# Loads moved ahead of the phases that use them, and the first attention group worked off in two query halves

## The chip, the cores and the metric

One core of a Trainium2 chip runs the whole program. The metric is the device time of one execution in microseconds (us), the median of three. Five engines work side by side: TensorE (PE; its weight loads are PEld), VectorE (DVE), ScalarE (ACT), GpSimd (POOL) and SyncE (SP), which here issues nearly all transfers. ACT can issue transfers too, on a queue of its own.

## The reference

Four sequences of 1024 tokens, 256 wide, in float32. Two layers, each a mixer and a feed-forward part; what matters here is the first layer:

```
# L0 attention, 16 heads of 16, causal, with an ALiBi slope for each head
att = softmax(q @ k.T / 4 + slope * tril(j - i) + causal)     # 1024 x 1024 for each head and sequence
x1  = x + (att @ v) @ W_proj + b_proj
# L0 ffn: two layers, each
h   = shift_token(z);  q, k, v = split(h @ wqkv)              # 8 heads of 64
q, k = rotary_xpos(l2norm(q) * q_scale, l2norm(k) * k_scale)
z1  = z + local_attention(q, k, v) @ wo                       # 128 queries see their block and the one before
h   = shift_token(z1);  a, g = split(layernorm(h) @ w1 + b1)
z   = z1 + (a * gelu(g)) @ w2 + b2
```

After it come the second layer's selective scan (a front of projections and a convolution, then the scan) and a mixture of 32 experts. Before each part stands a normalisation.

## The kernel before, in words

The kernel is a row of phases, each with on-chip buffers, semaphores and a block of its own: `phase_qkv` (A), `phase_attention` (B), then twice `phase_window` (D) and `phase_feed_forward` (E), then `phase_front` (F), `phase_scan` (H) and `phase_moe` (I). Tiles carry the letter of their phase in the profile (`B_probs`, `D_rope`). Between two phases all engines meet at a barrier, and what one phase hands to the next lies in device memory (`z`, `z1`, `q_parts`). So a phase can load its weights and its first tokens only after the barrier, and computes nothing till they are there.

Attention (B). Queries and keys are split into three bfloat16 parts, stacked on 96 partitions, with 4 more rows for the slopes and for the shift of the softmax. One group is 4 heads of one sequence; there are 16 groups. `load(g)` (lines 601 to 608) issues 17 transfers on SP: 12 of 128 KB for q and k, two of rows, the values (`v_raw`), `centre` and `key_bias`. All 17 count on one semaphore, so nobody starts on a group before its last transfer. A group has 48 units of maxima (`score` on PE, `reduce_max` on DVE, line 750) and 48 units of exponentials (`score_T` on PE, line 907, `Exp` on ACT, line 852). The exponentials need the row maxima as a shift: after the group's 48th maximum DVE works them out (`shifts`), PE turns them (`turn`, line 895), ACT copies them (line 844), and SP copies 4 rows for each head into `q` (`put_shift`, line 614). Every engine works its list strictly in order: PE does the 48 maxima of group 0 alone; from then on it takes an exponential unit and, beside it, the maxima of the next group, which keep a lead of up to 16. The shift of group g + 1 is turned before exponential 36 of group g. Every four exponentials PE also weighs the values (`weigh`, line 925). Two transposed halves of each group's result are stored as `yT` (line 626) and projected at fixed places, for sequence 2 before exponential 39 of group 11 (`project`, line 887; it waits for the stores of both halves it reads).

SP's list in B: `load(0)`, `load(1)`, `load(2)`, `put_shift(0)`, and then for each g: `load(g + 3)`, now and then x, the stores of `yT`, `put_shift(g + 1)`, and the stores of x1 and z.

Local attention (D) works 32 tiles of 128 tokens. At its start SP loads tiles 0 to 2, `ident`, `band`, `rope` and `wo`, ACT issues `wqkv` and `factor`. GpSimd builds the masks (lines 1124 to 1128) and multiplies all 8 blocks of the rotary table by the scales (line 1132) before it takes up the inverse norms of tile 0 (line 1137), which scale k (line 1181), which PE then turns (line 1358). In the steady part SP stores tile i and then loads tile i + 4.

Feed-forward (E) works 8 chunks of 512 tokens. SP loads chunk 0 first, then weights and chunk 1. In the first layer's E, `clear` (10 MB of zeros to `slots_x`) goes out on ACT's queue.

The front (F) starts with ACT waiting for all small weights, because it negates `dt_b` (line 2100) ahead of its first copy of the transposed tokens (line 2046).

## Time and profile before

| | |
|---|---|
| median of 3 runs | 3671.98 us (3669.59 to 3672.42) |
| the profiled execution: its own time, its span | 3675.01 us, 3673.2 us |
| mean granted clock of TensorE, share of full | 0.948 |
| TensorE, VectorE, ScalarE, GpSimd busy | 88%, 67%, 50%, 39% |
| attention's first matmul and last projection | 144.07 us, 740.8 us |
| D, E, D, E, F: first matmul | 757.2, 1271.3, 1532.4, 2048.1, 2310.4 us |

The span is from the first to the last instruction of the core. A start of a phase is seen as a stretch in which TensorE does nothing.

### The profile page before, as it was taken

The numbers are of one execution on the slowest core, as the hardware profiler recorded it, in microseconds if no ns is written. First come the engines' busy times: TensorE is split into PE (matmuls) and PEld (weight loads), VectorE is DVE, ScalarE is ACT, GpSimd is POOL, SyncE is SP. The second block draws the span as 40 slices with busy tenths as digits, with TensorE's granted clock in tenths as the row PEclk, the third lists the DMA queues.
The fourth block names the chain that finished last, engine by engine and source line by source line (L and its number), as shares of the span: only waits on it lengthen the run. The fifth ranks groups of instructions, "written<-read, shape, count | busy, mean of one in ns | idle before, by whom it ended". The sixth has DMA issues, their size and how long they took to land. (4 is left out here: it accounts for less than half of the span.)

```text
span 3673.2 us, 52297 instructions
## 1 busy us (share of the span) xinstructions
PE 3235.6 (88%) x18096; PEld 1975.8 (54%) x18096; DVE 2455.5 (67%) x4653; ACT 1849.0 (50%) x3943; POOL 1432.4 (39%) x993
## 2 busy tenths in 40 slices
PE   8599999879999799799999799798288888887798
PEld 4244444346666555466666455333256565655676
DVE  8488888547777422277777232398599999996633
ACT  2176776736666411166666211355377777774100
POOL 4101111122222211122222111134599999996533
PEclk9699999989999899899999899899699999999899
DMA  5956575120000241100000321343525151512873
GB/s 170 150 68 92 80 96 79 34 67 25 23 23 23 91 145 46 58 23 23 23 23 20 94 69 46 96 152 144 212 83 201 58 201 58 201 58 88 294 229 118
DMA packets 275715, 347.29 MB, mean 95 GB/s; under 512 B 70976, under 2 KB 206640, under 8 KB 274812
## 3 DMA queue, kind: packets, MB, share of 16 engines
q1 hardware_dynamic: 259596, 305.70, 30.5%
q10 hardware_dynamic: 10736, 25.94, 2.0%
q0 software_dynamic: 5120, 12.30, 0.9%
q8 instruction: 145, 2.38, 0.3%
q14 instruction: 118, 0.97, 0.1%
HBM read 227.72 MB, written 112.80 MB: 93 GB/s over the span
## 5 line engine op out<-in xcount | busy, mean ns | idle before, releaser
L2414 POOL TENSOR_TENSOR H_feed<-H_ndu,H_bs 128x1024 f32<-128x1024 f32 x256 | 595.6, 2372 | 7.0 <-DMA H_cs<-between_bc 4.0
L852 ACT ACTIVATE B_probs<-B_p_exp,B_key_bias 128x512 f32<-128x512 f32 (+3 forms) x768 | 394.8, 583 | 143.2 <-PE B_p_exp L910 112.8
L750 DVE TENSOR_REDUCE B_part_max<-B_p_max 128x1 f32<-128x512 f32 (+3 forms) x768 | 374.7, 546 | 83.3 <-PE B_p_max L874 80.8
L1286 ACT ACTIVATE D_probs<-D_scores,D_neg,D_rq 128x256 f32<-128x256 f32 x512 | 283.1, 573 | 255.7 <-DVE D_neg L1198 255.7
L2385 ACT ACTIVATE H_decay<-H_ndt,H_rate 128x1024 f32<-128x1024 f32 x256 | 287.9, 1125 | 198.7 <-DVE H_turning L2467 103.1
L871 PE MATMUL B_p_max<-B_k,B_q 100*128 100x512 bf16 (+3 forms) x768 | 256.7, 341 | 43.8 <-DMA B_key_bias<-in_key_bias 33.7
L1696 PE MATMUL E_p_ag<-E_hT,E_w 128*128 128x512 f32 x640 | 282.8, 601 | 2.1 <-ACT E_hT L1652 2.1
L2467 DVE TENSOR_TENSOR_SCAN H_turning<-H_decay,H_feed 128x1024 f32<-128x1024 f32 x112 | 253.5, 2275 | 22.9 <-POOL H_feed L2414 22.7
L2518 PEld LDWEIGHTS H_p_y<-H_minus,H_sT 128*128 128x128 f32 x1792 | 225.1, 200 | 75.6 <-ACT H_sT L2370 55.6
L2518 PE MATMUL H_p_y<-H_minus,H_sT 128*128 128x128 f32 x1792 | 233.5, 287 | 35.8 <-ACT H_sT L2370 35.8
L907 PE MATMUL B_p_exp<-B_q,B_k 100*128 100x512 bf16 (+3 forms) x768 | 250.1, 329 | 11.4 <-ACT B_probs L852 6.5
L1137 POOL TENSOR_TENSOR D_rnorm<-D_norm,D_power 128x8 f32<-128x8 f32 x64 | 106.2, 1659 | 380.3 <-DVE D_norm L1153 380.3
L1668 ACT ACTIVATE E_gated<-E_p_ag,E_b 128x512 f32<-128x512 f32 x96 | 62.6, 652 | 373.1 <-PE E_p_ag L1696 353.9
L2370 ACT ACTIVATE H_sT<-H_p_T,H_cT 128x128 f32<-128x128 f32 x896 | 242.9, 388 | 11.1 <-PE H_p_T L2508 11.0
L1341 PE MATMUL D_p_qk<-D_wqkv,D_hT 128*128 128x512 f32 x512 | 243.1, 618 | 1.1 <-ACT D_hT L1261 1.1
L1195 DVE CUSTOM_DVE_ANT_0 D_scores<-D_scores,D_mask 128x256 f32<-128x256 f32 x512 | 202.0, 457 | 56.0 <-PE D_scores L1368 55.7
L2467 DVE TENSOR_TENSOR_SCAN H_decay<-H_decay,H_feed 128x1024 f32<-128x1024 f32 x96 | 218.9, 2281 | 16.7 <-POOL H_feed L2414 16.6
L1141 POOL TENSOR_TENSOR D_rnorm<-D_norm,D_power 128x8 f32<-128x8 f32 x64 | 106.7, 1667 | 286.7 <-DVE D_norm L1153 286.7
L1696 PEld LDWEIGHTS E_p_ag<-E_hT,E_w 128*128 128x128 f32 x640 | 121.9, 192 | 155.2 <-issue 154.2
L1623 DVE SCALAR_TENSOR_TENSOR E_act_out<-E_p_ag,E_b,E_gated 128x512 f32<-128x512 f32 x96 | 67.7, 706 | 196.5 <-ACT E_gated L1668 196.5
L871 PEld LDWEIGHTS B_p_max<-B_k,B_q 100*128 100x128 bf16 x768 | 75.2, 98 | 221.5 <-DVE B_part_max L750 133.0
L2526 PE MATMUL H_p_y<-H_part,H_minus 128*128 128x512 f32 x384 | 184.5, 603 | 9.1 <-DVE H_part L2443 9.0
(269 smaller groups left out, 6857.8 us busy)
## 6 DMA issues: line engine op xcount, KB each, us to landing
H_bs<-between_bc SPq DMA_DIRECT2D x64, 512.0 KB, 7.7
H_cs<-between_bc SPq DMA_DIRECT2D x36, 512.0 KB, 8.4
B_q<-between_q_parts SPq DMA_DIRECT2D x96, 128.0 KB
B_k<-between_k_parts SPq DMA_DIRECT2D x96, 128.0 KB
between_slots_x<-E_clear ACTq DMA_DIRECT2D x4, 2570.0 KB
I_xe<-between_slots_x ACTq DMA_DIRECT2D x32, 257.0 KB, 4.0
D_base<-between_z SPq DMA_DIRECT2D x64, 128.0 KB
between_z<-D_z SPq DMA_DIRECT2D x64, 128.0 KB
```

The costliest lines, as they stand in the source:

```text
L750: nc.vector.reduce_max(part_max[:, g % 2, kc, qb, h:h + 1], p_max[:, use % 3, 0:keys], AX.X).then_inc(maxed, 1)
L852: nc.scalar.activation(probs[:, x % PROBS, skip:512], p_exp[:, n % SCORES, skip:512], ACT.Exp, bias=key_bias[:, g % SETS, kb - 4 * Q + 4, ...
L871: last = nc.tensor.matmul(p_max[:, use % 3, 0:keys], q[0:KR, u, h, qb * P:(qb + 1) * P], k[0:KR, u, h, 512 * kc:512 * kc + keys], start=Tr ...
L907: last = nc.tensor.matmul(p_exp[:, n % SCORES, skip:512], k[0:KR, u, h, kb * P:(kb + 1) * P], q[0:KR, u, h, 512 * Q + skip:512 * Q + 512], ...
L1286: last = nc.scalar.activation(probs[:, place[m], :, :].rearrange("p a b -> p (a b)"), scores[:, place[m], :, :].rearrange("p a b -> p (a b ...
L1341: last = nc.tensor.matmul(p_qk[:, m, :], hT[:, i % 2, k, :], wqkv[:, k, m * INNER:(m + 1) * INNER], start=k == 0, stop=k == KD - 1)
L1696: last = nc.tensor.matmul(p_ag[:, m % 2, n, :], w1[:, k, at:at + P], hT[:, i % 2, k, :], **flags)
L2370: last = nc.scalar.activation(sT[:, k % 2, h * HB + b, :], p_T[:, h, b, :], ACT.Copy, scale=cT[:, i % 2, h * HB + b, s:s + 1])
L2385: nc.scalar.activation(decay[:, n % 2, :], ndt[:, g % 2, :], ACT.Exp, scale=rate[:, m, s:s + 1]).then_inc(decayed, 1)
L2414: nc.gpsimd.tensor_tensor(feed[:, n % AHEAD, :], ndu[:, g % 2, :], bs[:, s, :], ALU.mult).then_inc(fed, 1)
L2467: nc.vector.tensor_tensor_scan(out, decay[:, n % 2, :], feed[:, n % AHEAD, :], 0.0, ALU.mult, ALU.add).then_inc(scanned, 1)
L2518: last = nc.tensor.matmul(p_y[:, h, b * P:(b + 1) * P], sT[:, k % 2, h * HB + b, :], minus[:, :], start=False, stop=False)
```

## The change

It has three parts.

1. Loads ahead. Two new classes own the buffers of D's and of E's weights and first tokens (`LocalAhead`, `FeedAhead`), which now outlive a phase. D's list (11 weight transfers and tiles 0 to 2) is issued by SP during attention, after `put_shift(11)`, and for the second layer after chunk 3 of E. E's list (18 weight transfers and chunks 0 and 1) is issued by SP in D after the store of tile 16. The waits at a phase's start are for these semaphores. In D GpSimd now does block 0 of the rotary table first, and the other seven, two at a time, after the inverse norms of tiles 0 to 3. In E the memset of `clear` comes after the first inverse deviation.
2. Group 0 of attention. q goes on SP's queue and k on ACT's, each as two halves of 512 tokens, with a semaphore for each half, and the values between the halves of q. PE starts at the first half. Only 24 maxima come first: 16 of the first query half (`OWN`), whose shift is made at once, and 8 of the second. Then come `turn`, the 16 exponentials of the first half with the other 24 maxima beside them, the second `turn`, and the 32 exponentials of the second half with two maxima each beside them. SP's list begins: group 0, `load(1)`, `put_half(0)`, `load(2)`, `put_half(1)`. The shift of group 1 is turned before exponential 44 of group 0 (`LATE_TURN`) and no longer before 36.
3. In F GpSimd negates `dt_b`, and ACT waits for it at its first `put_xs`.

```diff
-        stream = [("turn", 0, 0), ("turn", 0, 1)]
+        EARLY, OWN, LATE_TURN = 24, 4 * GH, 44
+        stream = [("turn", 0, 0)]
         for g in range(NG):
             for e in range(NE):
-                if e == TURN and g + 1 < NG:
+                if g == 0 and e == OWN:
+                    stream.append(("turn", 0, 1))
+                if e == (TURN if g else LATE_TURN) and g + 1 < NG:
                     stream += [("turn", g + 1, 0), ("turn", g + 1, 1)]
...
         def max_target(g, e):
             at = NE * g + e + 1
+            if g == 0:
+                return EARLY + 3 * at // 2 if e < OWN else NM + 2 * (at - OWN)
             return min(NG * NM, NM + at + min(LEAD, at * LEAD // NE))
...
+            def load_first():
+                for half, done in ((0, first_half), (1, second_half)):
+                    cols = slice(512 * half, 512 * half + 512)
+                    for n, part in enumerate((0, 0, 1, 1, 0, 2)):
+                        sp.dma_start(q[HD * n:HD * n + HD, 0, :, cols], ...).then_inc(done, 16)
+                    if half == 0:
+                        sp.dma_start(q[96:KR, 0, :, :], T["q_rows"]).then_inc(done, 16)
+                        values(0)
+            def put_half(half):
+                sp.wait_ge(exped, (turned[0] if half else 0) + 1)
+                for h in range(GH):
+                    sp.dma_start(q[96:KR, 0, h, 512 * half:512 * half + 512], shift_rows[32 * h:32 * h + 4, 0, half, :]
+                                 ).then_inc(q_shifted, 16)
...
-            load(0)
+            load_first()
             load(1)
+            put_half(0)
             load(2)
-            put_shift(0)
+            put_half(1)
...
+                if g == NG - 6:
+                    sp.wait_ge(first_row, 16)
+                    sp.wait_ge(z_stored[0], 16)
+                    local.load(sp, T, 0)
...
# phase_window, SP
+                if i == TILES // 2:
+                    sp.wait_ge(first_row, 16)
+                    for u in range(2):
+                        sp.wait_ge(stored[u], 16 * 4)
+                    feed.load(sp, T, layer)
# phase_window, GpSimd
-            pool.wait_ge(rope_loaded, 16 * 7)
-            for b in range(BLOCKS):
-                nc.gpsimd.tensor_tensor(rope[:, b, :, :], rope[:, b, :, :], factor[:, :, :], ALU.mult
-                                        ).then_inc(rope_ready, 1)
             for i in range(TILES):
                 inverses(i)
+                for b in range(2 * i + 1, min(2 * i + 3, BLOCKS)):
+                    tables(b)
...
# phase_feed_forward, SP
+                if i == 3 and not last_layer:
+                    sp.wait_ge(stored[0], 16)
+                    local.load(sp, T, layer + 1)
...
# phase_front
+            nc.gpsimd.tensor_scalar(dt_b[:, :], dt_b[:, :], -1.0, None, ALU.mult).then_inc(bias_ready, 1)
-            act.wait_ge(small_loaded, 16 * (TAPS + 3 + XT))
-            nc.scalar.mul(dt_b[:, :], dt_b[:, :], -1.0).then_inc(bias_ready, 1)
-            act.wait_ge(bias_ready, 1)
```

## Rows read from the trace of the kernel before

**Rows 1.** Sums by window: length, busy of PE, PEld, DVE, ACT, POOL, clock, DMA, GB/s.

```profile
110.30:144.10 33.80, 0.08 (x2) 0.06 (x2) 2.05 (x5) 0.00 (x0) 6.75 (x6) 0.57 0.98 162
174.90:218.20 43.30, 39.93 (x292) 18.34 (x293) 31.98 (x70) 27.28 (x51) 1.05 (x1) 0.90 0.48 58
...
1518.80:1532.40 13.60, 0.03 (x3) 0.04 (x1) 1.22 (x1) 0.00 (x0) 1.17 (x4) 0.60 0.52 180
```

**Rows 2.** Timeline of the start of D, first layer: start, length, instruction, idle before.

```profile
748.73 0.36 SPq L1097 DMA_DIRECT2D D_ident<-in_ident  x1
757.23 0.45 PE L1333 MATMUL D_p_hz<-D_ident,D_base 128*128 128x128 f32 x1 [16.39 <-DMA D_before<-between_z]
762.86 0.69 DVE L1153 TENSOR_REDUCE D_norm<-D_square 128x8 f32<-128x512 f32 x1 [18.11 <-ACT D_square L1266]
764.06 5.96 POOL L1132 TENSOR_TENSOR D_rope<-D_rope,D_factor 128x256 f32<-128x256 f32 x8 [3.04 <-DMA D_factor<-in_k_scale]
769.98 1.63 POOL L1137 TENSOR_TENSOR D_rnorm<-D_norm,D_power 128x8 f32<-128x8 f32 x1
772.07 0.69 DVE L1181 TENSOR_TENSOR D_kr<-D_ksum,D_rnorm 128x512 f32<-128x512 f32 x1 [4.67 <-POOL D_rnorm L1139]
777.71 3.53 PE L1368 MATMUL D_scores<-D_qkT 64*128 64x256 f32 x16 [1.19 <-ACT D_qkT L1277]
```

**Rows 3.** Timeline of the starts of E, both layers: first issue, first statistics.

```profile
1259.70 0.37 SPq L1528 DMA_DIRECT2D E_h<-between_z  x1
1266.36 1.41 DVE L1604 BATCH_NORM_STATS2 E_stats<-E_h 128x6 f32<-128x256 f32 x4 [9.53 <-DMA E_h<-between_z]
2036.79 0.38 SPq L1528 DMA_DIRECT2D E_h<-between_z  x1
2043.12 1.41 DVE L1604 BATCH_NORM_STATS2 E_stats<-E_h 128x6 f32<-128x256 f32 x4 [9.20 <-DMA E_h<-between_z]
```

**Rows 4.** Timeline of the start of F.

```profile
2310.41 1.09 PE L2135 MATMUL F_p_T<-F_ident,F_xn 128*128 128x128 f32 x4 [13.99 <-DVE F_xn L1973]
2316.32 0.59 ACT L2046 COPY F_xT<-F_p_T 128x512 f32<-128x512 f32 x1
```

**Rows 5.** Timeline of group 0 of attention: group 1's values, shift rows, first exponential.

```profile
160.85 0.61 POOL L685 COPY B_v<-B_v_raw 128x512 f32<-128x512 f32 x1 [16.25 <-DMA B_key_bias<-in_key_bias]
170.93 2.61 SPq L614 DMA_DIRECT2D B_q<-B_shift_rows  x4
175.62 0.69 ACT L852 ACTIVATE B_probs<-B_p_exp,B_key_bias 128x512 f32<-128x512 f32 x1 [4.72 <-PE B_p_exp L910]
```

**Rows 6.** Sums by window, maxima alone (line 750): length, DVE busy, clock, DMA, GB/s.

```profile
144.10:168.00 23.90, 23.06 (x48) 0.57 1.14 127
188.40:218.20 29.80, 20.77 (x44) 0.94 0.23 21
```

**Rows 7.** Stores of yT, issue to landing, from 226 to 245 us and from 577 to 580 us.

```profile
DMA to landing us min/median/max: 2.4/6.1/10.2
...
L626 SPq DMA_DIRECT2D B_yT<-B_yn x4: 507/590/594, 577.2 to 579.0; - x4
DMA to landing us min/median/max: 2.0/2.2/2.4
```

**Rows 8.** Timeline: shift rows of group 11, first load of group 14, projection for sequence 2.

```profile
551.03 2.50 SPq L614 DMA_DIRECT2D B_q<-B_shift_rows  x4
559.50 0.35 SPq L601 DMA_DIRECT2D B_q<-between_q_parts  x1
584.33 1.51 PE L887 MATMUL B_p_max<-B_w,B_yT 128*128 128x256 f32 x6
```

**Rows 9.** Transfers of the stretch from 749 to 767 us.

```profile
DMA packets 4304, 4.26 MB, mean 237 GB/s; under 512 B 1104, under 2 KB 4048, under 8 KB 4304
```

**Rows 10.** Timeline in the steady part of D: a tile's load, and PE taking up a tile.

```profile
1033.20 0.43 SPq L1090 DMA_DIRECT2D D_base<-between_z  x1
1055.34 0.27 PE L1333 MATMUL D_p_hz<-D_ident,D_base 128*128 128x128 f32 x1
```

More of the change, by code:

```diff
@@ L574, in phase_attention @@
         max_use, unit_use = {}, {}
-        for n in range(NM):
+        for n in range(EARLY):
             max_use[n] = n
@@ L838, in _ @@
         def _(act):
+            for half, done in ((0, first_half), (1, second_half)):
+                cols = slice(512 * half, 512 * half + 512)
+                for n, part in enumerate((0, 1, 0, 1, 2, 0)):
+                    act.dma_start(k[HD * n:HD * n + HD, 0, :, cols], T["k_parts"][part_rows(0, part), cols]
+                                  .rearrange("(h d) t -> d h t", h=GH)).then_inc(done, 16)
+                if half == 0:
+                    act.dma_start(k[96:KR, 0, :, :], T["k_rows"][0:4, :, :]).then_inc(done, 16)
             for n, (kind, g, at) in enumerate(stream):
@@ L891, in turn @@
             def turn(n, g, half):
-                pe.wait_ge(shift_ready, g + 1)
+                pe.wait_ge(shift_ready, g + 2 if g else half + 1)
                 reached(pe, exped, n - SCORES + 1)
@@ L1078, in starts @@
             return i % BLOCKS == 0
-        def loads(i):
-            return sum(3 if starts(j) and j else 2 for j in range(i % 4, i + 1, 4))
         @block.sync
@@ L1508, in reached @@
                 eng.wait_ge(sem, value)
-        def starts(i):
-            return i % PER_SEQ == 0
-        def loads(i):
-            return sum(4 if starts(j) else 2 for j in range(i % 2, i + 1, 2))
         rest_transfers = 2 if last_layer else 1
@@ L1589, in _ @@
                 if i == 0:
-                    pool.wait_ge(b2_loaded, 16 * CT)
+                    if not last_layer:
+                        nc.gpsimd.memset(clear[:, :], 0.0).then_inc(clear_ready, 1)
+                    pool.wait_ge(feed.weights, WEIGHTS)
                 pool.wait_ge(rest_loaded[u], 16 * rest_transfers * (i // 2 + 1))
@@ L3065, in tables, with __init__, total, loads @@
             **attention_tables(), **rope_tables(), **slot_tables()}
+class LocalAhead:
+    WEIGHTS = 11
+    def __init__(self, nc, ctx):
+        sb = lambda name, shape: ctx.enter_context(nc.sbuf_tensor(f"LA_{name}", shape, F32))
+        self.ident = sb("ident", [P, P])
+        self.band = sb("band", [P, 2, P])
+        self.wqkv = sb("wqkv", [P, KD, 3 * INNER])
+        self.wo = sb("wo", [P, INNER // P, DIM])
+        self.factor = sb("factor", [P, 4, LD])
+        self.rope = sb("rope", [P, SEQ // P, 4, LD])
+        self.base = sb("base", [P, 4, DIM])
+        self.before = sb("before", [P, 4, P])
+        self.weights = nc.alloc_semaphore("LA_weights")
+        self.loaded = [nc.alloc_semaphore(f"LA_loaded_{u}") for u in range(4)]
+    def total(self, i):
+        return sum(3 if j % (SEQ // P) == 0 and j else 2 for j in range(i % 4, i + 1, 4))
+    def loads(self, layer, i):
+        return layer * self.total(TILES - 4 + i % 4) + self.total(i)
+    def load_tile(self, sp, T, i):
+        u, tok = i % 4, i * P
+        sp.dma_start(self.base[:, u, :], T["z"][tok + 1:tok + 1 + P, :]).then_inc(self.loaded[u], 16)
+        if i % (SEQ // P) == 0 and i:
+            sp.dma_start(self.before[1:P, u, :], T["z"][tok + 1:tok + P, P:DIM]).then_inc(self.loaded[u], 16)
+            sp.dma_start(self.before[0:1, u, :], T["zeros"][0:1, 0:P]).then_inc(self.loaded[u], 16)
+        else:
+            sp.dma_start(self.before[:, u, :], T["z"][tok:tok + P, P:DIM]).then_inc(self.loaded[u], 16)
+    def load(self, sp, T, layer):
+        sp.dma_start(self.ident[:, :], T["ident"][:, :]).then_inc(self.weights, 16)
+        sp.dma_start(self.band[:, :, :], T["band"].rearrange("a p n -> p a n")).then_inc(self.weights, 16)
+        sp.dma_start(self.wqkv[:, :, :], T["wqkv"][layer].rearrange("(k p) n -> p k n", p=P)).then_inc(self.weights, 16)
+        sp.dma_start(self.rope[:, :, :, :].rearrange("p b a d -> p b (a d)"),
+                     T["rope"][0:SEQ, :].rearrange("(b p) n -> p b n", p=P)).then_inc(self.weights, 16)
+        for n, name in enumerate(("q_scale", "k_scale")):
+            row = T[name][layer:layer + 1, :]
+            sp.dma_start(self.factor[:, 2 * n, :], row.broadcast_to([P, LD])).then_inc(self.weights, 16)
+            for side in range(2):
+                here, other = side * HALF_D, (1 - side) * HALF_D
+                sp.dma_start(self.factor[:, 2 * n + 1, here:here + HALF_D],
+                             row[:, other:other + HALF_D].broadcast_to([P, HALF_D])).then_inc(self.weights, 16)
+        sp.dma_start(self.wo[:, :, :], T["wo"][layer].rearrange("(k p) n -> p k n", p=P)).then_inc(self.weights, 16)
+        for i in range(3):
+            self.load_tile(sp, T, i)
```

267 lines of the change are left out of this document (136 added, 131 removed).

## The prediction

> **What bounds the kernel now.** I read the page first: TensorE is busy for 88% of the span, so in the steady stretches its list sets the pace, and time can be had only where it stands still. So I looked for the stretches without a matmul, and summed the engines over them by window. Between A and attention TensorE does nothing for 33.8 us, ahead of the second D for 13.6 us [rows 1]; the starts of the first D, both E and F look like the latter. In these windows TensorE's granted clock averages 0.57 to 0.60, so the work that follows starts at the lower level of 1.2 GHz. Then I read the timelines of these starts for what ended last. At D it is the transfer of the first tokens: the block's first issue is at 748.73, the first matmul at 757.23 [rows 2]. At E it is the chunk of tokens that DVE waits for: 1259.70 to 1266.36, and 2036.79 to 2043.12 [rows 3]. In attention it is first the 17th transfer of group 0, then the lone maxima, which keep DVE busy for 23.06 of 23.90 us (0.48 us each) while TensorE waits on it [rows 6], then the turn of the shift.
>
> **The starts of D.** After the change weights and tiles are on the chip at the barrier. I take TensorE's first matmul 0.45 us after the block's first instruction: 757.23 - 748.73 - 0.45 = 8.0 us gained. Behind it lies a second wait. GpSimd multiplies eight table blocks, 764.06 to 770.02, before the inverse norm that was ready to be worked at 763.55 (762.86 + 0.69); k is scaled at 772.07 [rows 2]. Now one block is done before the norm arrives, so the inverse starts at 763.6 instead of 769.98, 6.4 us earlier on the same scale. TensorE must first finish the projection of v and the turn of tile 1, which costs some 0.2 us of that, and I take off as much again for DVE: 6.0 us. From k's scaling to the first scores it is 5.6 us either way (777.71 - 772.07). So 14.0 us for this D. The second has the same list; its idle stretch of 13.6 us [rows 1] is shorter than the first's 16.4 [rows 2] only by what lies ahead of the barrier, so again 14.0. Bounds for a D: 8 (the table work hides nothing) and 18 (TensorE keeps the upper clock through the shortened gaps and saves a few us on the first tile). The cover for the seven later blocks is GpSimd's idle time in tiles 0 to 3: two blocks are 2 x 0.75 = 1.5 us (5.96 / 8 each) in a tile of some 15 us (32 tiles from 777.71 to 1259.70 [rows 2 and 3]); without it they would cost 6 us.
>
> **The starts of E.** 1266.36 - 1259.70 = 6.7 and 2043.12 - 2036.79 = 6.3 us of waiting, less 0.1 each for DVE's own start: 12.8 us together [rows 3]. Bounds 10 and 15. The memset of `clear` now comes behind the first inverse; ACT, which waits for it after its first `hT`, has nothing else to do before the first product: 0, at most 2 us.
>
> **F.** ACT's first copy of the transposed tokens starts at 2316.32, though TensorE was done at 2310.41 + 1.09 = 2311.50. It had waited for the small weights. Gain 4.8 us [rows 4]; the negation on GpSimd is one 128 x 4 instruction and is needed much later. Bounds 2 and 5.
>
> **What pays for it: the lists on SP's queue.** In attention, D's list follows `put_shift(11)`, issued from 551.03 for 2.50 us, so begins at about 553.6, and stands ahead of `load(14)`, issued from 559.50 [rows 8]. Transfers of one queue land behind one another: the stores of yT issued right behind a group's load needed up to 10.2 us to land, those issued on a drained queue 2.0 to 2.4 us [rows 7]. The list is 4.0 MB. At the 237 GB/s with which the same list came in at D's start [rows 9] it needs 16.7 us, at best some 13, so it is through at 567 to 571. Group 14's load then begins 7 to 11 us late, and behind it come the yT stores of group 11's first half, which the projection at 584.33 waits for [rows 8]. They landed at 579.0 + 2.2 = 581.2, so 3.1 us of the delay is slack: a stall of 4 to 8 us. I take 5. Bounds 0 (the queue drains faster) and 12. Next behind it is `put_shift(12)`, which has 10 us.
>
> In D, E's list (4 MB, 24 transfers) stands ahead of one tile's load. A load issued at 1033.20 is for the tile that TensorE takes up at 1055.34 [rows 10], 22.1 us later. The list takes 13 to 17 us by the rate above and lands some 4 us before it is missed: nothing, with up to 5 us for each D as the other bound. D's list in E has a chunk of 32 us as cover: nothing.
>
> **Group 0 of attention.** Before: maxima from 144.1 to 168.0 [rows 6], SP's shift issues at 170.93, first exponential 175.62 [rows 5], so the turn costs 7.6 us; the group's exponentials and 64 maxima end at 218.2 [rows 1]. After: the first half of q and k is 0.8 MB, so that at 127 GB/s [rows 6] and with other traffic between, PE starts at about 131 and has the 24 maxima by 144. Their shift is at SP by 146. But SP's list has `load(1)` ahead of `put_half(0)`, and group 0 and 1 together bring the same bytes as before. The last transfer of group 1 landed at 160.85 [rows 5], and the shift rows land right behind it, by the queue's behaviour above. First exponential at about 161.5. Its 16 exponentials with 24 maxima take 14 us (12.8 before, with 21 maxima [rows 6]); at 175.6 comes a second turn of 6.7 us (half the rows to turn and copy), since nothing else is listed for TensorE there; exponential 16 starts at 182.3. Then 64 maxima at 0.487 us are 31.2 us of DVE, with 2.5 us of its other work and start: 216. DVE, not TensorE, is the bound here, as the 20.8 us for 44 maxima already hint [rows 6]. The late turn of group 1 leaves only four exponentials of cover and costs 1 us. End 217 against 218.2: I count 2 us gained, since two queues may bring group 1 a little earlier. Bounds: if the rows landed at once, at 149, exponential 16 would wait for group 2's load (about 174) and the group would end at 208, 10 us gained; if the DVE-bound part stretches like before's (29.8 us for 44 maxima), 5 us lost.
>
> The Trainium skill ("DMA: Bandwidth & Descriptors", "Rules for kernel authors") says that a second issuing queue brings no bandwidth, since all run on the same 16 engines. No row here shows two queues on these 16-partition transfers. By that rule group 1 still lands at 160.85 and this term is 1 us; if two queues did double the rate for their 0.8 MB, it would be 3 to 4 us.
>
> **The sum.** D 28.0, E 12.8, F 4.8, group 0 2.0, together 47.6; less the stall of 5.0 is 42.6. For fewer stretches at the lower clock in D I add 1.4, which is the middle of 0 and some 3: 44.0. The profiled execution took 3675.0, which gives 3631.0; the median lies 3.0 below it, so 3628.
>
> **Rivals.** (a) The shift rows do not wait behind `load(1)` (few rows, few engines), and yT neither: group 0 gains 10 and there is no stall, 13 more: 3615. For it: in calm stretches such rows land within 4 us. Against: the 10.2 us [rows 7]. (b) D gains only its first wait, since TensorE or DVE is late anyway before the first scores: 12 less, 3640. The row of 5.96 us [rows 2] speaks against it. (c) Queues bite deeper: 12 us at the projection, 5 at each D's list: 17 less, 3645. The 22.1 us against 17 speak against it, narrowly. (d) Slower: D's list clogs SP's queue in attention. The stall is the list's end less 559.5 less 3.1 us; it eats the 49 us of all gains once the list ends at 612, that is at under 70 GB/s over 58 us. Were it to last 65 us, the time would be 3679. Rows 9's 237 GB/s for the same transfers is against it. (e) No change, because the starts only move the wait to the first tile's or chunk's next transfer: 3672; against it stands that all of the first three tiles are in the list.
>
> **How the numbers follow.** Forecast 0.56, (a) 0.14, (b) 0.12, (c) 0.12, (d) 0.03, (e) 0.03. The forecast's own spread is 3619 to 3637; 3612 to 3643 takes in (a), (b) and most that lies between, leaving about 2 in 10. What this kernel's measurement can tell from no change is 0.2%, 7 us: faster 0.94, same 0.03, slower 0.03.
>
> **What the profile after would show.** In D: the first matmul within 1 us of the block's first instruction, one `D_rope` instruction before the first `D_rnorm`, and the first scores some 14 us after the first matmul (20.5 before). In E: statistics at once. In F: the copy right behind the transposes. In attention: maxima at 131, first exponential near 161 with SP's shift issues at 146, a second hole of 6 to 7 us before exponential 16, DVE over 90% busy from 183 to 216; and a hole of about 5 us in front of the projection in group 11. Wrong would be: shift rows landing at 149, no hole at the projection, or tiles 19 to 21 of D waiting for their tokens.

## The result: faster, by less than forecast

The changed kernel takes 3646.0 us (median of 5 runs, 3636.7 to 3651.4), the kernel before 3672.0 us (5 runs, 3669.6 to 3679.1): a ratio of 0.9926, with a 95% interval of 0.9907 to 0.9944. The forecast was 3628 us with a range of 3612 to 3643, so the sign was right and the time lay 3 us outside the range. The profiled execution went from a span of 3673.2 to 3644.2 us: 29 us gained where 44 were forecast. By the medians the gain is 26 us, since before the change the profiled execution lay 3.0 us above its median, and after it the profiled execution is the median.

First what came out as forecast. These are lines of the timeline of the changed kernel: the start of the first D, the first E, the second E, and F. They answer to [rows 2], [rows 3] and [rows 4].

```profile
755.71 0.45 PE L1364 MATMUL D_p_hz<-LA_ident,LA_base 128*128 128x128 f32 x1 [8.12 <-PEq L83]
756.76 0.72 POOL L1160 TENSOR_TENSOR LA_rope<-LA_rope,LA_factor 128x256 f32<-128x256 f32 x1
...
761.54 1.64 POOL L1175 TENSOR_TENSOR D_rnorm<-D_norm,D_power 128x8 f32<-128x8 f32 x1 [2.68 <-DVE D_norm L1193]
...
769.26 3.36 PE L1399 MATMUL D_scores<-D_qkT 64*128 64x256 f32 x14 [1.19 <-ACT D_qkT L1308]
...
1254.96 1.40 DVE L1585 BATCH_NORM_STATS2 E_stats<-FA_h 128x6 f32<-128x256 f32 x4 [2.86 <-PEq L83]
...
1258.32 4.38 POOL L1570 MEMSET E_clear<- 128x5140 f32 x1
1262.66 2.37 POOL L1573 TENSOR_TENSOR E_rest<-E_rest,FA_b 128x1024 f32<-128x1024 f32 x1
...
1258.40 7.43 DVE L1597 TENSOR_SCALAR E_hn<-FA_h,E_mean_var,E_rstd 128x256 f32<-128x256 f32 x4 [1.62 <-POOL E_rstd L1567]
...
1265.98 1.94 PE L1663 MATMUL E_p_T<-FA_ident,E_hn 128*128 128x128 f32 x8 [14.34 <-DVE E_hn L1597]
...
2021.05 1.38 DVE L1597 TENSOR_SCALAR E_hn<-FA_h,E_mean_var,E_rstd 128x256 f32<-128x256 f32 x4 [1.61 <-POOL E_rstd L1567]
...
2022.58 1.73 PE L1663 MATMUL E_p_T<-FA_ident,E_hn 128*128 128x128 f32 x7 [8.27 <-DVE E_hn L1597]
...
2283.83 1.09 PE L2113 MATMUL F_p_T<-F_ident,F_xn 128*128 128x128 f32 x4 [14.38 <-DVE F_xn L1952]
...
2284.96 0.58 ACT L2025 COPY F_xT<-F_p_T 128x512 f32<-128x512 f32 x1 [25.28 <-PE F_p_T L2113]
```

Ahead of the first D TensorE stands still for 8.12 us in place of 16.39, and from its first matmul to the first scores it is 769.26 - 755.71 = 13.55 us in place of 20.48. In F the copy follows the transposes at once. In both E the statistics start with the block. But the idle stretch ahead of E falls only in the second: 8.27 us there, 14.34 in the first. There the four `E_hn` instructions took 7.43 us and not 1.38, over nearly the same time (1258.40 to 1265.83, against 1258.32 to 1265.03) in which GpSimd fills `clear` and adds to `rest`.

Second, the two lists on SP's queue. Timeline lines of D's list in attention, then of E's list in the first D, each with the first matmul that came late by it:

```profile
554.17 2.07 SPq L3083 DMA_DIRECT2D LA_wqkv<-in_wqkv  x1
...
567.83 0.43 SPq L635 DMA_DIRECT2D B_q<-between_q_parts  x1
...
579.08 9.52 SPq L662 DMA_DIRECT2D B_yT<-B_yn  x8
...
590.04 3.32 PE L944 MATMUL B_p_max<-B_w,B_yT 128*128 128x256 f32 x7 [5.91 <-issue]
...
1024.49 0.33 SPq L3141 DMA_DIRECT2D FA_ident<-in_ident  x1
...
1037.53 5.19 SPq L3131 DMA_DIRECT2D FA_h<-between_z  x1
...
1044.07 0.74 SPq L3073 DMA_DIRECT2D LA_base<-between_z  x1
...
1048.88 0.33 PE L1364 MATMUL D_p_hz<-LA_ident,LA_base 128*128 128x128 f32 x1 [2.23 <-DMA LA_before<-between_z]
```

Group 14's load is issued at 567.83, 8.3 us later than in [rows 8], and the stores of yT begin 11.3 us later, since SP also took 2.9 us longer over the load and x. SP is busy with the eight stores for 9.52 us, but 5.10 of them are the first store alone, and the same store held SP for 4.94 us in the kernel before. The changed kernel, then the kernel before:

```profile
579.08 5.10 SPq L662 DMA_DIRECT2D B_yT<-B_yn  x1
```
```profile
567.82 4.94 SPq L626 DMA_DIRECT2D B_yT<-B_yn  x1
```

The last four stores go out from 586.2 to 588.0 (577.2 to 579.0 in [rows 7]: 9.0 us later) and land 1.9 to 2.3 us after their issue, so the last one at about 590.0. The projection starts at 590.04, after a wait of 5.9 us. The profile names no releaser for this wait ("issue"); that it is the stores follows from this landing and from the second experiment. Once issued, the stores land as fast as on a drained queue. The view of the DMA issues from 577 to 590 us (number, KB each, median us from issue to landing) has them:

```profile
B_yT<-B_yn SPq DMA_DIRECT2D x8, 32.0 KB, 2.3
```

In D, SP needs from 1024.49 to 1044.07 for E's list, 5.19 us of it for one single transfer. The load of tile 20 stands behind it: it is issued at 1044.07, and TensorE, which asks for the tile at 1048.88 - 2.23 = 1046.65, waits for 2.2 us.

Third, group 0 of attention, in timeline lines and in the sums by window (length, then busy time with the number of instructions of PE, PEld, DVE, ACT, POOL, then clock, DMA share, GB/s). They answer to [rows 5] and [rows 6].

```profile
142.00 0.59 ACT L897 CAST B_shift_rows<-B_p_exp 128x512 bf16<-128x512 f32 x1 [34.73 <-PE B_p_exp L952]
142.61 2.61 SPq L651 DMA_DIRECT2D B_q<-B_shift_rows  x4
...
153.30 0.61 POOL L726 COPY B_v<-B_v_raw 128x512 f32<-128x512 f32 x1 [18.74 <-DMA B_key_bias<-in_key_bias]
...
155.06 0.61 PE L966 MATMUL B_p_exp<-B_q,B_k 100*128 100x512 bf16 x1 [13.10 <-DMA B_q<-B_shift_rows]
...
172.54 0.58 ACT L897 CAST B_shift_rows<-B_p_exp 128x512 bf16<-128x512 f32 x1 [3.08 <-PE B_p_exp L952]
...
176.78 0.61 PE L966 MATMUL B_p_exp<-B_q,B_k 100*128 100x512 bf16 x1 [4.27 <-DMA B_q<-B_shift_rows]
```
```profile
130.10:142.00 11.90, 9.28 (x48) 4.03 (x48) 10.83 (x28) 0.01 (x1) 0.61 (x1) 0.64 1.11 165
142.00:155.80 13.80, 0.74 (x3) 0.39 (x4) 0.00 (x0) 0.58 (x1) 0.61 (x1) 0.50 1.03 117
155.80:177.40 21.60, 14.35 (x98) 6.27 (x97) 13.99 (x28) 8.80 (x17) 0.00 (x0) 0.82 0.40 40
177.40:216.50 39.10, 35.25 (x229) 15.12 (x227) 30.55 (x68) 19.93 (x34) 1.05 (x1) 0.85 0.46 63
```

The first scores come 13.10 us, and exponential 16's 4.27 us, behind a turn, with TensorE idle. Group 1's first exponential stands at 218.4 us, where it stood before (218.2). In the stretches that hold or follow the two holes TensorE's granted clock is 0.50 and 0.82 to 0.85, that is wholly or in part 1.2 GHz.

From the first exponential to group 1's first it is 62.6 us (155.8 to 218.4), and was 42.5 before (175.62 to 218.17). The new order lost the 20 us that the earlier start had won.

### The profile page after: what moved, and what is told of

Read it like the earlier page. It is cut to its first block and busy times, and to the rows that moved or that the text cites. A ratio compares the mean times of both kernels' runs of the same rounds, so it can differ in the third digit from the quotient of the medians.

```text
span 3644.2 us, 52320 instructions
## 1 busy us (share of the span) xinstructions
PE 3237.4 (89%) x18096; PEld 1980.4 (54%) x18096; DVE 2456.9 (67%) x4657; ACT 1848.5 (51%) x3942; POOL 1430.8 (39%) x992
## 5 line engine op out<-in xcount | busy, mean ns | idle before, releaser
L1677 PE MATMUL E_p_ag<-E_hT,FA_w 128*128 128x512 f32 x640 | 283.8, 603 | 1.9 <-ACT E_hT L1633 1.9
L928 PE MATMUL B_p_max<-B_k,B_q 100*128 100x512 bf16 (+3 forms) x768 | 254.6, 338 | 34.2 <-DMA B_q<-in_q_rows 20.1
L1649 ACT ACTIVATE E_gated<-E_p_ag,FA_b 128x512 f32<-128x512 f32 x96 | 62.5, 651 | 373.6 <-PE E_p_ag L1677 354.4
L1372 PE MATMUL D_p_qk<-LA_wqkv,D_hT 128*128 128x512 f32 x512 | 240.2, 612 | 0.9 <-ACT D_hT L1292 0.9
L1677 PEld LDWEIGHTS E_p_ag<-E_hT,FA_w 128*128 128x128 f32 x640 | 122.1, 193 | 155.7 <-issue 152.0
L1604 DVE SCALAR_TENSOR_TENSOR E_act_out<-E_p_ag,FA_b,E_gated 128x512 f32<-128x512 f32 x96 | 67.8, 707 | 199.4 <-ACT E_gated L1649 199.4
```

Source lines behind the costliest of these rows:

```text
L928: last = nc.tensor.matmul(p_max[:, use % 3, 0:keys], q[0:KR, u, h, qb * P:(qb + 1) * P], k[0:KR, u, h, 512 * kc:512 * kc + keys], start=Tr ...
L1372: last = nc.tensor.matmul(p_qk[:, m, :], hT[:, i % 2, k, :], wqkv[:, k, m * INNER:(m + 1) * INNER], start=k == 0, stop=k == KD - 1)
L1677: last = nc.tensor.matmul(p_ag[:, m % 2, n, :], w1[:, k, at:at + P], hT[:, i % 2, k, :], **flags)
```

## The experiments

Times of single profiled executions are given where only a stretch matters. Kernels of one group ran on one chip. Beside them the kernel before had medians of 3689.9 (one run), 3677.5 (7) and 3680.4 (7), so whole times are compared only within a group, and stretches across all traces. The first six experiments have one execution each: 3637.1, 3641.1, 3637.6 and 3625.1 us (memset behind `hn`; list two groups later; list in four; maxima first) beside 3689.9, and 3636.0 and 3643.2 (rows by ACT; tables at once) beside 3677.5.

**E's memset behind `hn`.**

```diff
                 if i == 0:
                     if not last_layer:
+                        pool.wait_ge(hn_ready, 1)
                         nc.gpsimd.memset(clear[:, :], 0.0).then_inc(clear_ready, 1)
```

> The kernel after, with one wait more: in the first E, GpSimd fills `clear` only after DVE has written the first `hn` (it waits for `hn_ready`), and adds `b2` to `rest` behind that. In the kernel after, the four `hn` instructions of the first E took 7.43 us (1258.40 to 1265.83) with GpSimd's memset of `clear` (1258.32, 4.38 us) and its add (1262.66, 2.37 us) over the same time; in the second E, without a `clear`, they took 1.38. Theory A (GpSimd's work beside it slows DVE): `hn` takes 1.4 us, the idle stretch of TensorE ahead of the first E falls from 14.3 to 8.3 us, like the second E's. Theory B (something else is slow in the first E, as its transfers of `rest` that land then): `hn` stays at about 7.4 us and the stretch at 14.3. By A the time is 6 us under the kernel after, by B the same. The memset ends some 1.5 us later than before the edit, with ACT's first product not yet there: nothing.

The view of one source line (duration in ns as min/median/max, first and last start) of the changed kernel, and then of this one:

```profile
L1597 DVE TENSOR_SCALAR E_hn<-FA_h,E_mean_var,E_rstd x4: 400/1410/4444, 1258.4 to 1265.4; 128x256 f32<-128x256 f32 x4
```
```profile
L1598 DVE TENSOR_SCALAR E_hn<-FA_h,E_mean_var,E_rstd x4: 406/407/413, 1256.1 to 1257.0; 128x256 f32<-128x256 f32 x4
```

TensorE's idle stretch is 8.29 us: theory A, to the tenth. Narrower windows of the same view have the four one by one: the first, 4.44 us, is as long as the memset (4.38), the second, 2.42, as long as the add (2.37), and the last two take 0.40 each, when GpSimd is through (it ends at 1265.03, they at 1265.83). So they did not run evenly slower beside GpSimd: the first two stood as long as GpSimd's instructions lasted.

**D's list two groups later.**

```diff
-                if g == NG - 6:
+                if g == NG - 4:
```

> The kernel after, with D's list issued behind the shift rows of group 13 (g of 12) in place of group 11's. In group 12 and 13 no projection waits for stores that lie behind it until group 15, and no load of a group follows. Theory A (the list on SP's queue holds the yT stores back): the idle stretch of 5.9 us ahead of the projection in group 11 goes, the 32 last exponentials of group 11 take 25.7 us as before in place of 33.9, and attention ends 8 us earlier, unless the shift rows or stores of groups 13 and 14 become late (up to 3 us). Theory B (the stall has another origin, such as the projection's own place after the early loads): it stays, and attention ends as in the kernel after. By A 8 us under the kernel after, by B the same.

Theory A. TensorE waits for no issue in that stretch, group 11's exponentials from number 16 on take 27.0 us up to group 12's first, as before (35.2 in the changed kernel), and groups 12 to 15 take what they took (37.4, 32.1, 30.2, 29.3). From group 1's first exponential to the last of attention it is 8.1 us less than in the changed kernel.

**E's list in four parts.** Each `load` of the list takes a part; parts 0 to 3 are issued behind the stores of tiles 16 to 19.

```diff
-                if i == TILES // 2:
+                if TILES // 2 <= i < TILES // 2 + feed.PARTS:
...
-                    feed.load(sp, T, layer)
+                    feed.load(sp, T, layer, i - TILES // 2)
```

> The kernel after, with E's list in both D cut in four: identity, gains and w1 at tile 16, b1, w2 and b2 at tile 17, chunk 0 at tile 18, chunk 1 at tile 19. In the kernel after tile 18 of each D took 18.55 and 18.38 us where all others take 14.87 to 15.2, and SP issued the list from 1024.49 to 1044.07. Theory A (the list ahead of tile 20's load is too long): both tiles go back to 14.9 us, 7 us in all, since the longest part has 1.7 MB and takes under 10 us of the 22 that a tile's load has. Theory B (the same bytes in any pieces slow the tiles' transfers): tiles 18 to 22 together still lose 3 to 4 us for each D. By A 7 us under the kernel after, by B the same.

Theory A: tile 18 takes 14.9 us in both D, and TensorE waits for no tile. From the first scores to the end D takes 477.7 and 477.2 us, in the changed kernel 482.4 and 480.9. That is 8.4 us, of which the two tiles are 7.2; the rest lies within the scatter of a D (480.4 and 477.5 us for the second one in two traces of the kernel before).

**Group 0's maxima first.** 16 maxima, turn of the first half, 32 maxima, turn of the second half, exponentials.

```diff
-        EARLY, OWN, LATE_TURN = 24, 4 * GH, 44
+        EARLY, OWN = 48, 4 * GH
...
-                if g == 0 and e == OWN:
+                if g == 0 and e == 0:
                     stream.append(("turn", 0, 1))
...
             put_half(0)
-            load(2)
             put_half(1)
+            load(2)
```

> The kernel after, with group 0's exponentials no longer between the maxima of its second half: TensorE makes 16 maxima, the turn of the first half's shift, the other 32 maxima, the turn of the second half, and then exponentials with one or two maxima of group 1 each, by the order of the kernel before. SP has both halves' shift rows ahead of group 2's load. Loads of group 0 stay early and in two halves. Theory A (the hole of 13.1 us that TensorE has while the first rows are under way is where maxima are to be made, and DVE's list of 88 maxima behind the first exponential is what took the gain back): maxima end at 130.1 + 48 x 0.49 = 153.6, the first exponential is still at 156 since its rows land no earlier, exponential 16 about 13 us later, as before, and the first exponential of group 1 at 156 + 42.6 = 198 to 202, against 218.4 in the kernel after and 218.2 before: 16 to 20 us gained. Theory B (group 1 and its values land too late, or the later groups take it back because TensorE waits for group 2's load, now issued about 11 us later): under 8 us gained at the end of group 2.

Sums by window, to the first exponential, to exponential 16, to group 1's first:

```profile
142.00:158.60 16.60, 14.03 (x49) 4.03 (x50) 14.79 (x33) 0.56 (x2) 0.61 (x1) 0.50 0.42 45
158.60:170.60 12.00, 11.81 (x93) 6.05 (x90) 8.89 (x20) 8.10 (x17) 0.00 (x0) 0.88 0.76 96
170.60:201.00 30.40, 25.77 (x197) 10.56 (x198) 23.97 (x53) 18.79 (x35) 1.05 (x1) 1.00 1.04 110
```

Theory A: group 1 starts at 201.0, 17.4 us earlier, and keeps it to the end of attention. DVE now works 14.79 us in the hole in which it did nothing, so 44 maxima and not 64 are left beside the last 32 exponentials, and TensorE runs them at the full granted clock (1.00 against 0.85). How much of the gain the clock is, no run separates; in [rows 6] the same 44 maxima took 29.8 us at 0.94, here 30.4 at 1.00. This is nearly the order of the kernel before, begun earlier: the first exponential stands at 158.6 in place of 175.6, and 42.4 us (42.5 before) lie between it and group 1's first.

**Rows issued by ACT.**

```diff
                     nc.scalar.copy(shift_rows[...], p_exp[...]).then_inc(exped, 1)
+                    if n == 0:
+                        act.wait_ge(exped, 1)
+                        for h in range(GH):
+                            act.dma_start(q[96:KR, 0, h, 0:512], shift_rows[...]).then_inc(q_shifted, 16)
```

> The kernel after, with the first half's four shift-row transfers of group 0 issued by ACT, behind its own copy, and no more by SP behind group 1's load. All else stands, the second half's rows by SP behind group 2's load too. In the kernel after they were issued at 142.61 and TensorE took up the first scores at 155.1. Theory A (the rows queue behind group 1's load, which is on the same queue): from ACT's queue, empty since 130, they land 2 to 4 us after their issue and the first exponential comes at 146 to 149, in place of 155.8. Exponential 16 then waits for the second half's rows behind group 2's load, at 172 to 177, and group 1's first exponential comes at 214 to 219: little or nothing gained in the sum. Theory B (the 16 DMA engines are full with group 1's bytes whatever the queue, busy share 1.03 from 142 to 155.8): the rows land near 153 again and the first exponential stays at 155.

Timeline lines: ACT's issue, GpSimd's copy that waits for the last transfer of group 1, the first exponential.

```profile
142.86 2.55 ACTq L903 DMA_DIRECT2D B_q<-B_shift_rows  x4
...
155.27 0.61 POOL L726 COPY B_v<-B_v_raw 128x512 f32<-128x512 f32 x1 [19.74 <-DMA B_key_bias<-in_key_bias]
158.60 0.69 ACT L912 ACTIVATE B_probs<-B_p_exp,B_key_bias 128x512 f32<-128x512 f32 x1 [15.78 <-PE B_p_exp L976]
```

Theory A falls. From a queue of its own the 4 KB rows still land behind group 1's load, and now, it seems, behind a part of group 2's too, which SP issues from 141.56: the first exponential is 3 us later than with the rows from SP's queue, where theory B had it at the same time. Group 1's first exponential comes at 221.4.

**All tables at once.** GpSimd makes D's eight products ahead of the tiles, as before; the loads stay early.

```diff
-                for b in range(2 * i + 1, min(2 * i + 3, BLOCKS)):
-                    tables(b)
...
+            for b in range(BLOCKS):
+                tables(b)
```

> The kernel after, with all eight products of D's tables on GpSimd at once before the tiles, as in the kernel before; the early loads stay. It tells how much of D's gain comes from the order of the tables: in the kernel after, first matmul to first scores is 13.55 us, in the kernel before 20.5. Theory A (both parts of the prediction's term hold, 8 for the loads and 6 for the tables): first matmul still 0.2 us behind the block's start, first scores 19 to 20.5 us behind the first matmul, so 6 to 7 us lost for each D, 13 in all. Theory B (with the tables on the chip at the barrier GpSimd is through with them before it is missed): under 3 us lost for each D, since it starts 8 us earlier on the scale of the block.

```profile
754.85 5.52 POOL L1160 TENSOR_TENSOR LA_rope<-LA_rope,LA_factor 128x256 f32<-128x256 f32 x8 [0.18 <-issue]
760.32 2.09 POOL L1176 TENSOR_TENSOR D_rnorm<-D_norm,D_power 128x8 f32<-128x8 f32 x1
```

Theory B: first matmul to first scores is 768.50 - 752.22 = 16.28 us, 2.7 more than in the changed kernel (2.2 in the second D), and not 6 to 7. The eight products start 2.6 us behind the first matmul, in the kernel before 6.8 (764.06 - 757.23), since their tables are there.

**The kernel before again.**

> The kernel before once more, for a second trace of it. The last stage, whose code the change does not touch, took 284.0 us from its first to its last matmul in the one trace of the kernel before, and 287.1 to 288.3 us in five traces of kernels with the change. Theory A (this is the scatter of that stage, and the one trace was a lucky one): 286 to 289 us here. Theory B (the change moves something that this stage depends on): 284 us again.

The last stage took 284.8 us here: below the 286 to 289 of theory A. But twelve traces of kernels with the change or a part of it have 284.3 to 288.3, so theory B, by which the change sets the higher value, does not hold either. That is mostly scatter; that both traces of the kernel before are at its lower end may be chance. In this trace the first E, which had taken 247.6 us, took 256.7, so a single profiled execution can be 9 us off.

**The mends together, and a tighter order for group 0.** Besides the three mends: eight maxima behind the first turn, two with each exponential, the second turn ahead of exponential 12, first rows by ACT, second rows ahead of group 2's load.

```diff
-        EARLY, OWN, LATE_TURN = 24, 4 * GH, 44
+        EARLY, OWN, SECOND, LATE_TURN = 24, 4 * GH, 12, 40
...
-                return EARLY + 3 * at // 2 if e < OWN else NM + 2 * (at - OWN)
+                return EARLY + 2 * at if e < SECOND else min(NM + 2 * (at - SECOND), 112)
```

> The kernel after with the three mends together (`clear` behind `hn`; D's list behind group 13's shift rows; E's list in four parts) and a new order for group 0: 16 maxima, the turn of the first half, 8 maxima while its rows are under way (issued by ACT), exponentials 0 to 11 with two maxima each, the turn of the second half ahead of exponential 12 (rows by SP ahead of group 2's load), and two maxima with each exponential from there until 64 are made. Theory A (the mends are worth 6 + 8 + 7 us, and group 0 lost its gain to the two holes and the slow stretch after the second): the first exponential near 145, no hole before exponential 16 over 2 us, the first exponential of group 1 at 188 to 196, so 22 to 30 us for group 0; in all 43 to 51 us under the kernel after, 3595 to 3605. Theory B (DVE bounds group 0 from 130 on, 112 maxima at 0.49 us and its other work, with slower maxima while TensorE is at the lower clock): group 1's first exponential at 200 or later, no better than with the maxima first (201.0), and in all 3605 to 3615.

3612.0 us (4 runs, 3610.8 to 3614.3), ratio to before 0.9818 (0.9786 to 0.985). Theory B by both its numbers, with group 1's first exponential at 208.2. That DVE bounds the stretch is not shown: from 171.0 to 208.2 it was busy for 29.79 of 37.2 us. The rows, issued at 139.77, let the first exponential start at 149.39, behind the last transfer of group 1 once more (GpSimd's copy at 147.91), and the order with exponentials between is 7 us slower than the maxima first.

**Group 0 as before, the early loads kept.** Its load, maxima, turn and exponentials are the code of the kernel before.

```diff
-            load_first()
+            load(0)
             load(1)
-            put_half(0)
             load(2)
-            put_half(1)
+            put_shift(0)
```

> The kernel after with group 0 of attention wholly as in the kernel before (one load of 17 transfers on SP's queue, 48 maxima, one turn of both halves, then exponentials with maxima of group 1 alone). The early loads of D and E, E's and F's changes stay. In the traces the first exponential of group 1 stands at 218.2 before and at 218.4 after, whatever happened ahead of it. Theory A (the new order of group 0 gains nothing): group 1's first exponential at 217.5 to 218.5, the time within 3 us of the kernel after run beside it, so all of the 26 us come from the early loads. Theory B (the new order helps somewhere later, as by the state in which it leaves the queues): over 5 us slower than the kernel after.

**The mends with the maxima first**, and the same with its second turn three exponentials later:

```diff
-                if g == 0 and e == 0:
+                if g == 0 and e == 3:
                     stream.append(("turn", 0, 1))
```

> The three mends of the early loads (`clear` behind `hn`; D's list behind group 13's shift rows; E's list in four parts) with group 0's 48 maxima first, the second 32 in the first rows' hole. In single runs the parts were worth 6.0, 8.2, 7.2 and 17.4 us. Theory A (they add up): 38.8 us under the kernel after run beside it, group 1's first exponential at 201, attention's last exponential 26 us earlier than in the kernel after. Theory B (they share something, as a stall that moves): under 32 us.

> The kernel of the row above, with the turn of group 0's second half listed ahead of exponential 3 in place of exponential 0. With the maxima first, the first half's rows had landed at 151.8, but the first exponential stood behind the turn, whose copy was at 158.04. Theory A (the list alone held it): first exponential at 155.5 to 156.5 in place of 158.6, group 1's first exponential 2 to 3 us earlier, so 198 to 199. Theory B (DVE bounds the stretch, or the turn's wait for DVE's shift only moves behind exponential 2): group 1's first exponential at 200 to 201, the time as the row above within 1 us.

> The kernel after, unchanged, on the same chip as the three others, so that they can be compared with it: 3636 to 3651 by its five runs. Its trace tells how far the stall of 5.9 us ahead of group 11's projection (group 11's last 32 exponentials took 33.9 us with it; 28 to 36 us in traces of kernels that have the same list at the same place) and the last stage's 287.1 us scatter. Theory A (both are scatter of transfers): 28 to 36 and 284 to 288. Theory B (fixed by the program): 34 and 287 again.

These four ran on one chip, 4 runs each:

| kernel | median us | range | ratio to before, 95% |
|---|---|---|---|
| changed kernel again | 3644.6 | 3644.0 to 3645.1 | 0.9909, 0.9877 to 0.9941 |
| group 0 as before | 3638.1 | 3636.2 to 3643.0 | 0.9893, 0.986 to 0.9927 |
| mends, maxima first | 3606.4 | 3604.7 to 3607.3 | 0.9806, 0.9774 to 0.9838 |
| and turn at 3 | 3607.4 | 3605.7 to 3609.0 | 0.9809, 0.9777 to 0.9841 |

With group 0 as before, group 1 starts at 219.3 (220.1 in the changed kernel beside it), and the kernel is no slower: the gain of the change comes from its early loads and F's edit. It is even 6.5 us faster, where theory A allowed 3, and the ranges of the four runs do not touch. In the traces the difference lies mostly in places that the edit does not touch: 4.0 us in the stall of group 11 and 3.3 in the first D, both of which scatter from trace to trace. Whether the new order of group 0 has a part in it, as by the times at which it leaves the queues, stays open; it gained nothing. The mends add up: 38.2 us under the changed kernel, 38.8 expected. That they agree so well is in part luck, since two of the parts, the stall and the late tiles, scatter by more than that. The changed kernel's second trace has 36.4 us for group 11's exponentials from number 16 on (35.2 in the first) and 284.7 us for the last stage (287.1), which is theory A: both scatter. The later turn brings the first exponential to 155.6, as theory A has it, but group 1 starts at 200.4 against 200.8, and group 2 1.2 us later: theory B.

The wait of TensorE ahead of the projection in group 11, in the eight traces that have D's list there and were not meant to mend it:

| trace | wait us |
|---|---|
| changed kernel, and again | 5.9, 7.5 |
| memset behind `hn`; list in four; maxima first | 3.6, 7.2, 4.7 |
| rows by ACT; tables at once; group 0 as before | 1.1, 2.5, 3.1 |

The mean is 4.5 us. In both traces of the kernel before and in those with the list two groups later there is none. The extra time of tile 18 scatters too: 0 to 4.5 us for each D where the list is whole, none where it is in four.

## Why the prediction fell short, by its own steps

The median came out 18 us above the forecast (3646 against 3628). Of these, 3 us are the last step of the sum: the median was put 3.0 us below the profiled execution, as before the change, and this time the two were one. The other 15 us are the sum itself (44 against 29.0 in the profiled execution). Term by term:

- **Starts of D, 28.0 forecast.** Measured: idle stretch and first tile together went from 16.4 + 20.5 to 8.1 + 13.6 = 15.2 us gained, and in the second from 34.2 to 19.4, 14.8: 30.0. The sum was right to 2 us, its split was not. I gave 6 us to the order of the tables; it is worth 2.7 and 2.2, and the tables that are on the chip at the barrier give the rest. That the two came to about the same sum is luck. Rival (b) is out.
- **Starts of E, 12.8 forecast, 6.9 measured: the step that failed most.** The second gained 6.3 as forecast, the first 0.6. The step read "the memset of `clear` now comes behind the first inverse [...] 0, at most 2 us". I asked only who waits for the memset's result (ACT), not what runs beside it. Before, GpSimd had filled `clear` while DVE was waiting for its tokens; now it does so in the 7 us in which DVE has the only work that matters. The first experiment gives the 6.0 us back. The Trainium skill ("SBUF — State Buffer", "SBUF: two separate sides") says that DVE and GpSimd share a pair of ports, which is held for the whole of an instruction while the other engine blocks, if DVE's instruction is in a 2-port perf mode, or has two inputs in SBUF and GpSimd's reads SBUF. The 4.44 us of one `hn` beside a memset of 4.38, and 0.41 alone, agree with such a lock; that `hn` runs in a 2-port mode no row shows. Had I weighed it, the term would have been 6 us lower and the forecast 3634; the measured time lies outside the stated range all the same, and inside it if its upper end moves by 6 us too.
- **E's list in D, forecast "nothing, with up to 5 us for each D as the other bound", measured 3.7 and 3.5.** The 22.1 us of cover were right: 1046.65, when tile 20 was asked for, is 22.2 us after the list's start at 1024.49. The list was not. I took it at 237 GB/s, the rate of D's list at an idle start, so 13 to 17 us; SP needed 19.6 us to issue it, with 5.19 us in one transfer. And with 17 us for the list and "some 4 us" to spare I had left about 1 us for the tile's own transfers behind it: they were issued at 1044.07 and let TensorE go on at 1048.88, 4.8 us later. 19.6 and 4.8 are 24.4 us against 22.2. Cutting the list removes the loss. Over all traces with the whole list it is 0 to 4.5 us for each D, so that execution had nearly the upper end.
- **The stall in group 11, 5.0 forecast, 8.2 measured** (27.0 to 35.2 us for that stretch): a wait of 5.9, and some 2 us more behind it. The load was 8.3 us late against 7 to 11 forecast, and the stores stood behind it. They were not slow to land (2.3 us), they were late to be issued, the last four by 9.0 us: the 8.3 of the list, 2.9 more over the load and x, less some 2 us that SP had spent between the stores before, in part waiting for their data. The wait alone was near the 5 us; the 2 us behind it I did not have. Over eight traces the wait alone is 4.5 us on average. So this is a term that was mis-sized, within its bounds.
- **Group 0, 2.0 forecast, 0 measured.** The first exponential came at 155.8 and not at 161.5, since group 1's last transfer landed 7.5 us sooner than before (153.30 for the 160.85 of [rows 5]). Then the last stretch took 41.0 us where I had 34.7. DVE's maxima there cost 30.4 us as worked out, but DVE was busy for only 78% of it, not over 90: behind the second hole TensorE had a granted clock of 0.85 and was busy for 35.25 of 39.1 us. Between 155 and 217 us DVE stood waiting for TensorE's maxima 16 times, 13.9 us in all, so the two held each other up in turn. "DVE, not TensorE, is the bound here" was the wrong step.
- **The rows behind the load.** The time was nearly right, the reason wrong. I argued by "the queue's behaviour"; from another queue the rows landed no sooner. What fits is that they wait for the load's bytes on the DMA engines, whose share was 1.03, whatever the queue. The rule that the prediction weighed (the Trainium skill, "DMA: Bandwidth & Descriptors", "Rules for kernel authors": queues run on the same 16 engines) agrees with this. At the start of group 0 the outcome that I had tied to the rule, group 1 at 160.85, did not come: it was there at 153.30. But the rule need not be wrong for that. The sums by window from 125 to 130 us, changed kernel and kernel before, show the DMA engines about as busy (1.20 and 1.08) and half as many bytes again moved:

```profile
125.00:130.00 5.00, 0.00 (x0) 0.00 (x0) 1.26 (x4) 0.00 (x0) 0.00 (x0) 0.50 1.20 194
```
```profile
125.00:130.00 5.00, 0.00 (x0) 0.00 (x0) 0.40 (x3) 0.00 (x0) 0.00 (x0) 0.50 1.08 131
```

That points to the shape of the half loads, with rows of 1 KB in place of 2 KB, more than to the second queue. No run separates the two.

- **F, 4.8 forecast, 4.8 measured**: from the first transpose to the copy it is 1.1 us in place of 5.9. Ahead of it 0.4 us are lost.
- **The clock term, 1.4, and the rest.** It can't be seen: D behind its first scores took 3.7 and 0.5 us longer, which the list explains. The last stage took 3.1 us longer in this execution with no edit in it; its scatter is as large. I had left no room for such scatter in the sum.

Added up: 5.9 for E's starts, 4.2 for D behind its first scores (7.2 by the two lists, 3 of it hidden because the other tiles of the second D ran that much faster than in the one trace before), 1.4 for the clock term, 3.2 for the stall, 3.1 for the last stage, 2.2 for group 0: 20.0. Less 2.0 that D's starts gave more and 3.0 of small gains (1.7 in the rest of attention, 1.0 in the two E, 0.3 in F and behind it), it is the 15 us. Rival (c), the queues biting deeper, came nearest with 3645, in part by luck: its two losses came to 7.2 of its 10 us in D and 8.2 of its 12 in attention, and the memset, which it does not have, made up for the rest.

So what failed is, first, the term for E's starts (a memset put at nothing), then the term for E's list in D (put at nothing, 7.2 us), and, by 3.2 and 2.2 us, the sizes of the stall and of group 0.

What the experiments leave open: what holds SP's issue (a full queue is the likely reading, and no run measured it), and why the wait in group 11 scatters from 1.1 to 7.5 us. Other places for the memset, as in D, were not tried.

## What to carry to other kernels

When a load is moved ahead, look at what used to run during the wait that it removes: work that cost nothing there (a memset on GpSimd beside an idle DVE) now runs beside the work that matters, and has to be moved too. A list of early loads wants a place where the transfers queued behind it are not missed for longer than the whole list takes to issue, or it is cut into pieces of a tile's length. And when a hole has to be crossed, put the work of the engine that will bound the next stretch into it: 32 maxima in the hole were worth 17.4 us, while the order with exponentials between them started those 9 us earlier still (149.4 for 158.6) and ended 7 us later.

## What the runs showed of the hardware that was not expected

- GpSimd and DVE on SBUF: one 128x256 `tensor_scalar` of DVE took 4.44 us beside a GpSimd memset of 4.38 us, and a second one 2.42 us beside an add of 2.37; alone each takes 0.40 to 0.41.
- Four shift-row transfers of 4 KB from ACT's otherwise empty queue, with SP's loads under way, were followed by the first exponential 9.6 us (139.77 to 149.39) and 15.7 us (142.86 to 158.60) after their issue; the like takes 4.7 us in a calm stretch (170.93 to 175.62 in [rows 5]).
- Issuing is not free when much is under way: one transfer of E's list held SP for 5.19 us, where most others of the list took 0.3 to 0.6, and everything listed behind it waited. It was so before the change too: 4.94 us for one store of yT behind a group's load.
